# A decoder layer on one core: batch 1 of x also loaded with its features on partitions, and batch 1's first values computed ahead of batch 0's scores

## The reference

```python
x = x + attn(layernorm(x), Wqkv, bqkv, Wo, bo)          # one head, d = 256
x = x + matmul(fake_quant(layernorm(x)), fake_quant(ctx))
x = x + ffn(layernorm(x), c1_w, c2_w, w1, w2t)          # blockwise argmax picks the hidden units

def layernorm(x):  return (x - m) / sqrt(v + 1e-5)
def attn:          q, k, v = split(x @ Wqkv + bqkv); softmax(q k^T / 16) v @ Wo + bo
def fake_quant(x): q = clip(round(x / s + z), 0, 255);  return (q - z) * s
```

## Time and profile before

| | us |
|---|---|
| median of 3 runs (798.16 to 799.9) | 799.47 |
| the profiled execution's own time | 799.37 |
| its span, first to last instruction | 797.5 |
| PE busy | 786.5 (99%) |
| DVE / POOL / ACT busy | 592.7 / 433.4 / 249.4 |

### The profile page before, as it was taken

The page is one execution under the profiler, slowest core; times in us unless marked ns, Lnnn a source line. Parts: engine busy times, 40 slices in busy tenths (PEclk is TensorE's granted clock), DMA queues, the critical chain, the costliest instruction groups (busy, mean ns, idle before and its releaser), DMA issues.

```text
span 797.5 us, 11473 instructions
## 1 busy us (share of the span) xinstructions
PE 786.5 (99%) x3883; PEld 640.0 (80%) x3888; DVE 592.7 (74%) x963; ACT 249.4 (31%) x374; POOL 433.4 (54%) x265
## 2 busy tenths in 40 slices
PE   8999999999999999999999999999999999999998
PEld 7888887468788888888888888888888888888886
DVE  5655568877984878787777878787878777777864
ACT  5457567872321131212122120303121212212030
POOL 3935797675999954544525253445454443525240
PEclk9999999999999999999999999999999999999999
DMA  8126403000111011111111111101111111111104
GB/s 333 71 101 215 162 1 106 8 1 8 60 53 30 31 53 60 53 59 53 59 53 59 53 59 53 45 16 50 59 53 59 53 59 53 59 53 53 53 15 196
DMA packets 22615, 53.22 MB, mean 67 GB/s; under 512 B 4544, under 2 KB 6592, under 8 KB 22464
## 3 DMA queue, kind: packets, MB, share of 16 engines
q1 hardware_dynamic: 22448, 51.86, 18.9%
q10 hardware_dynamic: 144, 1.05, 0.4%
HBM read 48.70 MB, written 4.19 MB: 66 GB/s over the span
## 4 chain that ended last, share of the span: by engine, by line
PE 87%; DVE 8%; DMA 2%; POOL 1%; ACT 1%; issue 1%; SPq 0%; DVEq 0%
PE bank L1752 12%; PE bank L1753 12%; PE bank L1754 12%; PE bank L1657 11%; PE bank L1659 11%; PE bank L1658 11%; PE bank L1470 3%; PE bank L1472 3%; PE bank L1471 3%; PE bank L1611 2%; PE bank L1666 2%; PE bank L1648 2%; DMA x<-x_in 1%; PE bank L1627 1%; DVE stats L1024 1%; PE bank L1486 1%
## 5 line engine op out<-in xcount | busy, mean ns | idle before, releaser
L1752 PE MATMUL bank<-w_hi,h_hi 128*128 128x512 f32 x448 | 176.5, 394 | 1.5 <-DVE x L1258 1.5
L1753 PE MATMUL bank<-w_lo,h_hi 128*128 128x512 f32 x448 | 175.1, 391 | 0.0
L1754 PE MATMUL bank<-w_hi,h_lo 128*128 128x512 f32 x448 | 174.5, 390 | 0.0
L1261 DVE TENSOR_TENSOR x<-bank,x 128x512 f32<-128x512 f32 x208 | 133.5, 685 | 50.0 <-PE bank L1754 50.0
L562 POOL TENSOR_TENSOR lo_r<-r,slot 128x512 fp32r<-128x512 f32 x52 | 67.5, 1300 | 160.4 <-ACT slot L785 160.4
L1754 PEld LDWEIGHTS bank<-w_hi,h_lo 128*128 128x128 f32 x448 | 84.1, 188 | 18.0
L1752 PEld LDWEIGHTS bank<-w_hi,h_hi 128*128 128x128 f32 x448 | 84.1, 188 | 17.9 <-DVE x L1258 2.2
L1753 PEld LDWEIGHTS bank<-w_lo,h_hi 128*128 128x128 f32 x448 | 84.4, 188 | 15.2
L1657 PE MATMUL bank<-xT_hi,slot 128*128 128x512 f32 x240 | 95.0, 396 | 0.0
L1658 PE MATMUL bank<-xT_lo,slot 128*128 128x512 f32 x240 | 93.5, 390 | 0.0
L1659 PE MATMUL bank<-xT_hi,lo_r 128*128 128x512 f32 x192 | 74.8, 390 | 0.0
(11 more groups left out here) (203 smaller groups left out, 1600.3 us busy)
## 6 DMA issues: line engine op xcount, KB each, us to landing
r<-w SPq DMA_DIRECT2D x56, 256.0 KB, 3.4
w_raw<-w SPq DMA_DIRECT2D x28, 512.0 KB, 4.0
x<-x_in SPq DMA_DIRECT2D x8, 512.0 KB, 10.4
ctx_raw<-ctx_in SPq DMA_DIRECT2D x8, 512.0 KB, 4.0
xn<-ctx_in SPq DMA_DIRECT2D x8, 512.0 KB, 5.5
out<-x SPq DMA_DIRECT2D x7, 512.0 KB, 2.7
W_raw<-wqkv SPq DMA_DIRECT2D x6, 512.0 KB, 10.8
c_raw<-c SPq DMA_DIRECT2D x112, 16.0 KB, 2.0
```

What stands on the lines that cost most here:

```text
L1261: nc.vector.tensor_tensor(x[:, t, c], bank[unit_banks(g)[p]][:, :], x[:, t, c], ALU.add).then_inc(unit_added, 1)
L1752: nc.tensor.matmul(dst, h_hi[:, j, m], w2_hi[:, j, c], start=j == 0, stop=False)
L1753: nc.tensor.matmul(dst, h_hi[:, j, m], w2_lo[:, j, c], start=False, stop=False)
L1754: last = nc.tensor.matmul(dst, h_lo[:, j, m], w2_hi[:, j, c], start=False, stop=j == GJ - 1)
```

## The change

A new input `xT_in` holds batch 1 of x with features on partitions. SP loads it whole (2 MB, one DMA) into `xT_raw` behind x tiles 6 and 7. Batch 1 is no longer normalised by ACT nor transposed by PE. Instead `spread_rows(p)` (p = 0, 1: a pair of token tiles) transposes a column of `rstd` and one of `nmr`, each repeated 128 times, for each of the pair's two tiles, so that a PSUM bank (a new job "R") holds the factors of 256 tokens on every partition: 4 transposes a pair, 8 in all instead of 32. `norm_xT` on DVE multiplies and adds them, in two halves of 4 feature blocks x 256 tokens. ACT makes the high part (`hi_xT`), and POOL, not DVE, the low part (`lo_xT`). R(0) stands behind Q(0,0) and R(1) behind Q(0,1).

`V(1,0)` moves from behind Q(1,3) to ahead of S(0,0), on PE and in the list of jobs, and its steps on ACT and DVE move with it. The first context loads wait for Q(0,3) instead of the last transpose, and pieces 0 to 3 are scaled and rounded before the softmax of batch 0 instead of after it. On POOL `x + bo` of tile 4 stands between the two pairs, and of tiles 5 to 7 behind them.

```diff
-    jobs += [("Q", 0, 0), ("Q", 0, 1)] + both("T1", 4) + [("Q", 0, 2)] + both("T1", 5)
-    jobs += [("Q", 0, 3)] + both("T1", 6) + both("T1", 7)
+    jobs += [("V", 0, 1), ("Q", 0, 0), ("R", 0), ("Q", 0, 1), ("R", 1), ("Q", 0, 2), ("Q", 0, 3), ("V", 1, 0)]
     jobs += [("S", 0, i) for i in range(4)]
-    jobs += [("Q", 1, c) for c in range(4)] + both("V", 1)
+    jobs += [("Q", 1, c) for c in range(4)] + [("V", 1, 1)]
...
+            sp.dma_start(xT_raw[:, :, :], xT_in).then_inc(xT_loaded, 16)
...
-            sp.wait_ge(mm_done, nth("T1", 7, 1) + 1)
+            sp.wait_ge(mm_done, nth("Q", 0, 3) + 1)
...
+            def lo_xT(p):
+                for h in range(2):
+                    pool.wait_ge(xT_hi_done, 2 * p + h + 1)
+                    at_pair = token_pair(p, h)
+                    nc.gpsimd.tensor_tensor(xT_lo[1][at_pair], xT_raw[at_pair], xT_hi[1][at_pair].bitcast(F32),
+                                            ALU.subtract).then_inc(xT_lo_done, 1)
+
+            add_bo(0, 1, 2, 3)
+            lo_xT(0)
+            add_bo(4)
+            lo_xT(1)
+            add_bo(5, 6, 7)
...
+            def norm_xT(p):
+
+                dve.wait_ge(mm_done, nth("R", p) + 1)
+                dve.wait_ge(xT_loaded, 16)
+                row = job_bank("R", p)[:, :].rearrange("p (s o m) -> p s o m", s=2, o=1)
+                scale, shift = (row[:, s].to_broadcast([P, 4, 2 * P]) for s in range(2))
+                for h in range(2):
+                    part = xT_raw[token_pair(p, h)]
+                    link(nc.vector.tensor_tensor(part, part, scale, ALU.mult))
+                    last = nc.vector.tensor_tensor(part, part, shift, ALU.add)
+                    if h == 0:
+                        last.then_inc(xT_normed, 1)
+                free(last)
...
+            def spread_rows(p):
+
+                pe.wait_ge(rstd_ready, nth_chain(0, TB) + 1)
+                take_bank("R", p)
+                for s, rows in enumerate((rstd, nmr)):
+                    for i in range(2):
+                        t, c = TB + 2 * p + i, (2 * s + i) * P
+                        last = nc.tensor.transpose(job_bank("R", p)[:, c:c + P],
+                                                   rows[:, t:t + 1].to_broadcast([P, P]), id_f[:, :])
+                last.then_inc(mm_done, 1)
...
@@ (ACT)
             hi_Q(0, 0)
             hi_Q(0, 1)
-            both(hi_T, 0, 4)
-            norm(0, 6)
+            hi_xT(0)
             hi_Q(0, 2)
-            both(hi_T, 0, 5)
-            norm(0, 7)
+            hi_xT(1)
             hi_Q(0, 3)
...
+            scale_ctx(0)
+            scale_ctx(1)
+            hi_V(1, 0)
+            scale_ctx(2)
+            scale_ctx(3)
             for i in range(TB):
                 exp(0, i)
...
                 scale_ctx(2 * c + 5)
-            hi_V(1, 0)
             scale_ctx(12)
@@ (DVE)
             lo_Q(0, 0)
+            norm_xT(0)
             lo_Q(0, 1)
-            lo_T(0, 4)
+            norm_xT(1)
             lo_Q(0, 2)
...
+            round_ctx(0)
+            round_ctx(1)
+            lo_V(1, 0)
+            round_ctx(2)
+            round_ctx(3)
             maxima(0)
...
                 round_ctx(2 * c + 5)
-            lo_V(1, 0)
             round_ctx(12)
@@ (PE)
             project_qk(0, 0)
+            spread_rows(0)
             project_qk(0, 1)
-            transpose_norm(0, 4)
+            spread_rows(1)
             project_qk(0, 2)
-            transpose_norm(0, 5)
             project_qk(0, 3)
-            transpose_norm(0, 6)
-            transpose_norm(0, 7)
+            pe.wait_ge(xT_lo_done, 2)
+            project_v(1, 0)
             for i in range(TB):
                 scores(0, i)
-            made("T1", NT - 1, 1)
+            pe.wait_ge(xT_lo_done, 4)
             for c in range(4):
                 project_qk(1, c)
-            project_v(1, 0)
             project_v(1, 1)
```

More of the change, by code:

```diff
@@ L96, in nth_chain, with decoder_layer @@
     return next(n for n, (r, first, count) in enumerate(CHAINS) if r == rnd and first <= t < first + count)
-def decoder_layer(nc, x_in, ctx_in, wqkv, bqk, bv, wo, bo, s1, z1, s2, z2, c1, c2, w1, w2, out):
+def decoder_layer(nc, x_in, xT_in, ctx_in, wqkv, bqk, bv, wo, bo, s1, z1, s2, z2, c1, c2, w1, w2, out):
     D = x_in.shape[2]
@@ L275, in decoder_layer @@
         normed = sem("normed")
+        xT_normed = sem("xT_normed")
+        xT_hi_done = sem("xT_hi_done")
+        xT_lo_done = sem("xT_lo_done")
         vbias_added = sem("vbias_added")
@@ L332, in job_pair, with token_pair @@
             return banks[:, n * BANK:(n + 2) * BANK]
+        def token_pair(p, h):
+            return (slice(None), slice(4 * h, 4 * h + 4), slice(2 * p * P, 2 * (p + 1) * P))
         def on_act(rnd, t):
@@ L500, in _, with add_bo @@
             pool.wait_ge(bias_loaded, 48)
-            for t in range(NT):
-                pool.wait_ge(normed, t + 1)
-                nc.gpsimd.tensor_tensor(x[:, t, :], x[:, t, :], bo_b[:, :], ALU.add).then_inc(bo_added, 1)
+            def add_bo(*tiles):
+                for t in tiles:
+                    if t < TB:
+                        pool.wait_ge(normed, t + 1)
+                    else:
+                        pool.wait_ge(mv_done, t + 1)
+                    nc.gpsimd.tensor_tensor(x[:, t, :], x[:, t, :], bo_b[:, :], ALU.add).then_inc(bo_added, 1)
+            def lo_xT(p):
[9 more added lines that the diff above has]
+            add_bo(5, 6, 7)
             def add_q2(b, i):
@@ L710, in hi_T, with hi_xT @@
                     job_bank(*job)[:, :].rearrange("p (k m) -> p k m", k=4), ACT.Copy).then_inc(hi_done, 1)
+            def hi_xT(p):
+                for h in range(2):
+                    if h == 0:
+                        act.wait_ge(xT_normed, p + 1)
+                    else:
+                        act.wait_ge(bank_free, nth("R", p) + 1)
+                    at_pair = token_pair(p, h)
+                    nc.scalar.activation(xT_hi[1][at_pair], xT_raw[at_pair], ACT.Copy).then_inc(xT_hi_done, 1)
             def hi_W(i, h):
@@ L858, in _ @@
             roots(0, 4)
-            norm(0, 4)
-            norm(0, 5)
             hi_Q(0, 0)
             hi_Q(0, 1)
-            both(hi_T, 0, 4)
-            norm(0, 6)
+            hi_xT(0)
             hi_Q(0, 2)
-            both(hi_T, 0, 5)
-            norm(0, 7)
+            hi_xT(1)
             hi_Q(0, 3)
-            both(hi_T, 0, 6)
-            both(hi_T, 0, 7)
+            act.wait_ge(qp_ready, 1)
+            scale_ctx(0)
[3 more added lines that the diff above has]
+            scale_ctx(3)
             for i in range(TB):
                 exp(0, i)
-            act.wait_ge(qp_ready, 1)
-            for i in range(4):
-                scale_ctx(i)
             for c in range(4):
@@ L1314, in _ @@
             nc.vector.tensor_copy(id_b[:, :], id_f[:, :]).then_inc(id_b_ready, 1)
-            for i in range(4):
-                round_ctx(i)
             for c in range(4):
@@ L1864 @@
         "x_in": x.reshape(nt, P, D),
+        "xT_in": x[1].T.reshape(kd, P, S).transpose(1, 0, 2),
         "ctx_in": ctx.reshape(B * kd, P, D),
```

17 lines of the change are left out of this document (8 added, 9 removed).

## The result

| | before | after |
|---|---|---|
| median, us | 799.37 (798.16 to 799.9) | 804.18 (803.51 to 804.82) |
| ratio, with its 95% interval | | 1.0059 (1.0043 to 1.0075) |
| the profiled execution's own time / its span | 799.37 / 797.5 | 804.16 / 802.1 |
| PE busy, us | 786.5 | 785.9 |

The account below looks back on a forecast made before the run. The prediction took PE, busy 786.5 of 797.5 us, to bound the kernel, nearly tied with the context chain. It summed 799.37 + 3.3 (later chain) + 1.8 (clock restart) = 804.5 us, range 801.6 to 807.2.

Parts of the forecast that it names:

- PE's own saving: PE before the scores: 32 transposes (3.60 us) go, eight with waiting add 1.2 (0.9 to 2.5); work falls 2.4 us.
- The cover of the new path: Load, DVE, ACT and POOL steps finish before V(1,0) and Q(1,0), with 4.7 and 8.7 us of cover; PE pays nothing.
- The shift: V(1,0) moved ahead makes Q(1,2) end 3.3 us later, at 78.0 instead of 74.7: -3.60 + 1.2 + 5.73.
- The chain: From Q(1,2) through context pieces to S(1,1): all 3.3 us later, S(1,1) at 98.9, PE's wait 6.5 us.
- Rival 3: Context chain shortens through faster POOL conversions and piece 14's load: 800.3 us without a fall of the clock; chance 0.07.
- The clock: After the 6.5 us wait at S(1,1) PE restarts slowly, costing 1.8 us, bounds 0 and 4.
- rival 1: The wait is there, but the clock holds or its fall hides in S(1,2)'s 0.2 us wait: 802.7 us; chance 0.26.
- Behind S(1,2): From S(1,2) to the end both traces should have the same length but for the slow stretch.
- The whole: Whole kernel: 799.37 + 3.3 + 1.8 = 804.5 us, chance 0.50.

Follow-up runs that it names:

- the kernel with the fillers: Changed kernel with 50 unused transposes of the identity on PE between S(1,0) and S(1,1): 802.11 us, ratio 1.0035.
- the last changed kernel: Changed kernel, Wo loaded before context pieces 14 and 15, ACT and DVE parts of O(0,0) and O(0,1) ahead of both pieces: 801.78 us.
- the ordered kernel: Changed kernel, V(1,1) and PT(0,i) parts ahead of context pieces 12 to 15, Wo's high part and batch 1's exponentials ahead of 15: 800.70 us.
- Wo first: Changed kernel, context pieces 14 and 15 loaded after Wo; Wo and exponentials ahead of piece 14, O(0,0) between 14 and 15: 800.94 us.
- with the ordered parts: Changed kernel, V(1,0) behind Q(1,3), small DVE operations behind `k_lo`, V(1,1), PT(0,i), Wo and exponentials ahead of last context pieces: 800.81 us.
- with the small operations late alone: Changed kernel, V(1,0) back behind Q(1,3), the tiny quantisation operations on DVE behind the low part of Q(0,3): 801.08 us.

## Why the prediction was right, step by step

It said 804.5 (801.6 to 807.2), and 804.18 was measured; the profiled execution took 804.16.

- **PE's own saving**, 3.60 - 1.2 = 2.4. The spreading is one row for each pair of transposes in the timeline:

```profile
32.18 0.43 PE L1539 MATMUL bank<-id_f,rstd 128*128 128x128 f32 x2
32.45 0.38 PE L1539 MATMUL bank<-id_f,nmr 128*128 128x128 f32 x2
```

  The eight cost 0.9 to 1.0 with their switches, no more than other transposes, and R(0) shows no wait: `nmr` ends at 32.13, just ahead. From the end of Q(0,0) to the first matmul behind Q(0,3) it is 17.33 us (32.18 to 49.51), before it was 19.97: the saving was 2.6, near the low bound of the cost.
- **The cover of the new path.** No wait ahead of V(1,0) (49.51) or Q(1,0). The load (issued at 10.96, 19.9 us to landing, so at 30.9; 29 was forecast) was there when `norm_xT` began at 33.73, each of its operations took 1.21 or 1.22 us (taken: 1.28), each ACT half 1.00 (1.05), each POOL half 2.38 (2.4), and POOL's additions ended at 59.93 (60).
- **The shift.** Q(1,2)'s high part starts at 77.25 instead of 74.75. This execution had all its early work 0.6 us sooner (Q(0,0) ends at 32.18, before it was 32.74; in the kernel with the fillers, the same up to there, it was 32.97, so this is chance), so the shift proper is 3.1, where 3.3 was forecast; V(1,0) has 5.75 of it (5.73).
- **The chain** from there to S(1,1) took 20.6 us instead of 20.9. Rival 3 had it up to 2.4 shorter. But POOL's conversions took 1.5 us each instead of 1.34 (2.99 for two, 4.01 for three before), and the load 4.57 instead of 5.48; it was that of piece 13, so that two scalings stand behind it where there had been one. S(1,1) at 97.85, with the early start taken out 98.45 (98.9 forecast); the wait 6.3 (6 to 7 forecast).
- **The clock.** Taken 1.8, from the program's start. The 18 matmuls from S(1,1) to O(0,0) took 6.16 us; at 0.228 us each and 0.11 for a start behind a wait they would have taken 4.2, so the lower level cost 1.9. Only 1.4 of that counts against the kernel before, which took 4.72 there. It waits for `pT_lo` ahead of S(1,2), and the starts around that wait are 0.48 us further apart than the pace; the slow stretch covers it. Timeline of PE before:

```profile
97.48 0.50 PE L1470 MATMUL bank<-k_hi,q_hi 128*128 128x512 f32 x1 [0.21 <-DVE pT_lo L1108]
...
100.33 0.39 PE L1470 MATMUL bank<-pT_hi,v_hi 128*128 128x512 f32 x1
```

  So the term was 0.4 too high as a difference between the two kernels; rival 1 had named the `pT_lo` wait as a place where a fall could hide. That the price at the restart, 1.9, lies so near 1.8 is in part luck: at the program's start the granted clock reads 1.00, so it is not shown that those transposes were slow for the same reason. As to the Trainium skill ("TensorE: Matmul & The Clock Gate", section "HAM oscillation — how this bites in real kernels"), this trace agrees: the move paid for the wait and for the restart.
- **Behind S(1,2)** I said that both traces would have the same length but for the slow stretch. That failed by 0.9 us: O(0,0) starts 3.7 us later than before, the span ends 4.6 later. Most of it is the wait for x, 1.3 us instead of 0.6. Timelines of DVE, of before and then of after:

```profile
133.48 1.29 DVE L1139 TENSOR_SCALAR xn<-xn 128x1024 f32<-128x1024 f32 x2
```

```profile
137.15 3.44 DVE L1183 TENSOR_SCALAR xn<-xn 128x1024 f32<-128x1024 f32 x2
```

  Two roundings of the normalised rows begin 0.23 us ahead of POOL's additions in both traces (133.48 and 133.71, 137.15 and 137.38), but beside them they take 1.29 us in one and 3.44 in the other, and x stands behind them. The kernel with the fillers and the old one with V(1,0) moved had the wait at 0.6, all the other kernels of the experiments at 1.3. What decides between the two is finer than these rows show and stays open.
- **The whole.** The forecast had +5.1. An earlier start by 0.6, a shorter shift and chain by 0.45 and 0.35 less for the clock take off 1.4, and 0.9 behind S(1,2) comes on: 4.6 us of span, and 0.2 outside it. The mechanism is the one forecast; that the total is within 0.3 us is luck, since errors of 1.4 and 0.9 us nearly cancel.

The prediction let PE's saving vanish inside one wait. That suggests that it could be had by taking the move back, and my expectation of that experiment said so; it was wrong. With V(1,0) back none of the saving is measurable (801.08, and 800.81 with another order).

## What to carry to other kernels

Work that an engine does between a producer and its consumer is a cover; before it is removed from a bound engine, ask which result was made behind it, and what is next when that one is late. Where the busiest engine already meets a chain of the others to within a microsecond, moving work ahead of that chain's head delays its end by nearly the whole of the moved work (5.2 of 5.7 us here), and shortening the busy engine may give only waits. The chain would have to be shortened first; no kernel here did that, so it is not shown that it pays. A wait of a few microseconds on TensorE has to be priced with the restart of its clock.

## What the runs showed of the hardware

- **The smallest operations can take over 2 us.** In the changed kernel the operations on 128x1 numbers with two operands in SBUF took 1.44, 2.19 and 2.25 us (from 45.79, 47.38 and 49.68) while POOL was busy with additions and subtractions; those between them with one operand took 0.14, and one of two operands that fell between two POOL operations (49.49) took 0.15. In the kernel before the same eight operations ran at 55 us, with POOL idle, in 0.14 to 0.16 each. The Trainium skill ("SBUF — State Buffer", section "Who interferes with whom") says that such a VectorE instruction and a GpSimd one that reads SBUF contend, under an exclusive lock. The rows agree: the three end at 47.23, 49.57 and 51.93, and POOL's instructions at 47.21 (44.80 + 2.41), 49.54 and 51.91 (47.16 + 4.75 for two). The wait lasts until POOL's instruction ends, however small VectorE's is.
- **Behind waits of about 2 to 3 us TensorE's clock fell in some executions and stayed in others.** In the profiled executions it fell behind waits of 6.3, 6.1, 3.0 (V(1,0) back, ahead of S(0,0)) and 2.3 us, and in the last changed kernel behind one of 1.8 us (PE works again from 148.16; the clock is 0.97 from 148 to 149, then 0.50), 6 us after one of 1.1. It stayed full behind 3.0 us (the ordered kernel, ahead of WO(0): 1.00 from 106 on) and behind 2.4 (Wo first). Of Wo first three executions of eleven kept the full clock, and they were 0.8 to 2.9 us faster than the rest; but only one, of the three, has a trace, so what the others waited for is not known. The same holds for the kernels with V(1,0) back, whose longest waits in the profiled executions are both 1.7: with the ordered parts the clock was full in all twelve executions, with the small operations late alone it fell in seven of twelve, and both traces are of executions at the full clock. What separates them was not tested.
